# A fused attention and expert stage: head of the schedule written out, attention products in 32-column quarters, one division moved

## The reference, cut to what matters

```python
# experts of the third layer (_L2_ffn_ref), E = 8, K = 2, hidden 512, capacity per expert
h = jax.nn.gelu(jnp.einsum('etc,ehc->eth', toks, fc1_w) + fc1_b[:, None, :], approximate=False)
y = toks + (jnp.einsum('eth,ech->etc', h, fc2_w) + fc2_b[:, None, :]) * layer_scale[:, None, :]
...
# attention of the fourth layer (_L3_xattn_ref), 16 heads of 8, top 32 of 128 keys
scores = jnp.einsum('bhqa,bhka->bhqk', q, k) * SCALE
cutoff = jax.lax.top_k(scores, TOP_K)[0][..., -1:]
w = jax.nn.softmax(jnp.where(scores >= cutoff, scores, -jnp.inf), axis=-1)
e = jnp.einsum('bhqk,bhka->bhqa', w, v)
```

## Time and profile before

| what | us |
|---|---|
| median of 3 timed runs | 3101.04 (3099.99 to 3103.3) |
| the profiled execution, its own time | 3106.62 |
| its span | 3104.8 |
| TensorE busy | 2850.7 (92%) |
| VectorE busy | 2030.3 (65%) |
| ScalarE busy | 1820.0 (59%) |
| GpSimd busy | 1427.0 (46%) |

### The profile page before, as it was taken

How to read it: one execution, slowest core, us unless ns; L and a number is a source line. 1 busy time by engine, 2 the same in 40 slices (tenths; PEclk the granted TensorE clock), 3 DMA queues, 4 the chain that set the end, 5 groups by cost and what they waited for, 6 DMA issues and landing times. The chain is left out here.

```text
span 3104.8 us, 70254 instructions
## 1 busy us (share of the span) xinstructions
PE 2850.7 (92%) x21784; PEld 2265.4 (73%) x21784; DVE 2030.3 (65%) x7995; ACT 1820.0 (59%) x5314; POOL 1427.0 (46%) x1744
## 2 busy tenths in 40 slices
PE   7999979987998989999999998999999996597999
PEld 6888854433775778888888777888888874486676
DVE  4444536764653456666666459999999999486433
ACT  5777734443553356666666567788888873353333
POOL 2122117762542434444444248788888876452000
PEclk9999979987998989999999899899999985597999
DMA  3000024433763311111111000000000000001000
GB/s 114 6 5 6 5 53 85 82 82 112 260 235 95 126 49 54 54 54 54 54 54 54 16 10 14 14 13 13 13 13 13 13 14 32 2 18 36 7 10 10
DMA packets 99460, 151.81 MB, mean 49 GB/s; under 512 B 11312, under 2 KB 39488, under 8 KB 98752
## 3 DMA queue, kind: packets, MB, share of 16 engines
q1 hardware_dynamic: 99296, 149.96, 16.5%
HBM read 103.33 MB, written 46.47 MB: 48 GB/s over the span
## 5 line engine op out<-in xcount | busy, mean ns | idle before, releaser
L1899 POOL TENSOR_TENSOR l2a_probs<-l2a_probs,l2a_inv 128x1024 f32<-128x1024 f32 x128 | 242.3, 1893 | 370.5 <-DVE l2a_inv L2065 370.5
L2010 ACT ACTIVATE l2a_probs<-l2a_s_ps,l2a_nm 128x256 f32<-128x256 f32 x512 | 236.1, 472 | 200.0 <-DVE l2a_nm L2041 200.0
L2760 DVE MAX8 l3a_top<-l3a_work 128x8 f32<-128x128 f32 x1536 | 314.1, 276 | 0.0
L2544 PEld LDWEIGHTS l3a_l2o_ps<-net_arena 128*128 128x128 f32 x2016 | 276.6, 222 | 39.0 <-issue 34.9
L2411 POOL TENSOR_SCALAR l3a_above<-l3a_score,l3a_top 128x128 f32<-128x128 f32 x504 | 294.1, 601 | 16.3 <-POOL l3a_probs L2416 7.2
L2544 PE MATMUL l3a_l2o_ps<-net_arena 128*128 128x128 f32 x2016 | 283.4, 308 | 10.6 <-ACT net_l1f_gate L2620 10.6
L2762 DVE MATCH_REPLACE8 l3a_work<-l3a_top,l3a_work 128x128 f32<-128x128 f32 x1024 | 268.8, 274 | 0.0
L2532 PE MATMUL l3a_l2h_ps<-net_cols,net_arena 128*128 (+1 forms) x1024 | 250.9, 388 | 12.9 <-ACT net_arena L2652 11.2
L2532 PEld LDWEIGHTS l3a_l2h_ps<-net_cols,net_arena 128*128 128x128 f32 x1024 | 184.9, 191 | 65.8 <-ACT net_arena L2652 24.5
L721 ACT ACTIVATE l0a_probs<-l0a_score_ps,l0a_nm 128x128 f32<-128x128 f32 x512 | 179.6, 382 | 73.6 <-DVE l0a_nm L770 73.6
L2652 ACT ACTIVATE net_arena<-l3a_l2h_ps,net_l2f_b 128x256 f32<-128x256 f32 x512 | 210.0, 492 | 16.6 <-PE l3a_l2h_ps L2532 13.7
(11 more groups left out here) (522 smaller groups left out, 7209.1 us busy)
## 6 DMA issues: line engine op xcount, KB each, us to landing
kv_ahead<-l1a_kept SPq DMA_DIRECT2D x128, 256.0 KB, 2.7
l0f_code<-code_rows SPq DMA_DIRECT2D x32, 512.0 KB, 11.5
l2a_kT<-kv_ahead SPq DMA_DIRECT2D x64, 256.0 KB, 2.6
l2a_v<-kv_ahead SPq DMA_DIRECT2D x64, 256.0 KB, 2.6
l1a_shift<-neg_top SPq DMA_DIRECT2D x16, 512.0 KB, 5.0
l1f_chosen<-mask_code SPq DMA_DIRECT2D x64, 128.0 KB, 3.1
keys_ahead<-l1f_keys_kept SPq DMA_DIRECT2D x32, 256.0 KB, 3.3
l3a_kT<-keys_ahead SPq DMA_DIRECT2D x32, 256.0 KB, 2.7
```

Of the source, the lines that this page charges most:

```text
L1899: pool.tensor_tensor(p[:, :, :], p[:, :, :], per_row(inv[c % 2][a][:, :, :].rearrange("p i o -> p (i o)"), KV), ALU.mult).then_inc(scaled, 1)
L2010: act.activation(probs[c % 2][a][:, 2 * i + odd, :], s_ps[a][odd][:, i * KV:(i + 1) * KV], ACT.Exp, bias=nm[c % 2][a][:, i, odd:odd + 1], ...
L2544: ins = pe.matmul(output_bank(u, x)[:, at:at + D], hidden[2 * x + n][:, i, j * P:(j + 1) * P], w2[:, expert(u, 2 * x + n), i, :], start=(i ...
L2760: ins = dve.max(t[:, step // 2, h, :], src)
```

## The change

- **Steps written out.** TensorE and ScalarE start the schedule at c = 0; what stood before it is now a hand-written order. `output` is split in halves of one expert each (`output_half`), which start between the hides. Hidden values of step 1 go to `probs` (`hidden_of`), which is unused then, and the first product of step 1 goes to `s_ps[0]`, so that both need not wait for step 0. `turn_rows` and `norm_rows` of the first group stand ahead of the outputs of step 2.
- **Quarters.** v gets 32 columns per head (8 values, a one, zeros). `apply` loads v and moves the turned probabilities: a head's output is 32 partitions x 128 columns, the four heads of a quarter lie in the four partition quarters of `ov_ps`. When all four are done, ScalarE copies the bank (`take_o`), TensorE transposes it back in four pieces into the same bank (`turn_out`), and `divide` reads it as before, 32 columns apart.
- **The end.** `divide` of tile 29 is done inside the last half of the last search, after its third of seven instructions per head; GpSimd's draining begins with `add_attention`; ScalarE's draining mixes `take_p` and `exps`.

The core of the diff:

```diff
         v_raw = [s.sb(f"v_raw{i}", [P, D]) for i in two]
-        v = [s.sb(f"v{i}", [P, H, DA + 1]) for i in range(4)]
+        WV = 32
+        v = [s.sb(f"v{i}", [P, H, WV]) for i in range(4)]
+        oT = s.sb("oT", [P, BANK])
         qT, kT = s.sb("qT", [P, P]), [s.sb(f"kT{i}", [P, Q4, P]) for i in two]
...
         prefix_ps, total_ps, early_ps = p_ps, ov_ps, s_ps[1]
-        o_ps = ov_ps[:, 0:H * (DA + 1)].rearrange("p (h d) -> p h d", h=H)
+        o_ps = ov_ps[:, :].rearrange("p (h d) -> p h d", h=H)
+        v_blank, o_taken, o_turned = s.sem("v_blank"), s.sem("o_taken"), s.sem("o_turned")
         k_loaded, v_loaded = ([s.sem(f"{n}_loaded{i}") for i in two] for n in "kv")
...
         def output_bank(u, x):
-            return early_ps if (u, x) == (0, 1) else o2_ps
+            return {(0, 1): early_ps, (1, 0): s_ps[0]}.get((u, x), o2_ps)
+
+        def hidden_of(q, u, x):
+            if isinstance(q, int) and (q, u) == (0, 1):
+                flat = probs[x // 2][:, :, :].rearrange("p h s -> p (h s)")
+                size = CHUNKS * WIDE
+                return flat[:, x % 2 * size:(x % 2 + 1) * size].rearrange("p (c n) -> p c n", c=CHUNKS)
+            return hidden[x]
...
                 for t in v:
-                    pool.memset(t[:, :, :], 1.0).then_inc(filled, 1)
+                    pool.memset(t[:, :, :], 0.0).then_inc(v_blank, 1)
+                for i, t in enumerate(v):
+                    pool.wait_ge(v_blank, i + 1)
+                    pool.memset(t[:, :, DA:DA + 1], 1.0).then_inc(filled, 1)
                 pool.wait_ge(filled, 4)
...
                                 (in_group(stage_weights, 0), -AHEAD), (add_attention, 3)], loops=0,
-                         draining=[(for_part(negate_max, 0), 1), (for_part(mask, 0), 1), (add_attention, 3)])
+                         draining=[(add_attention, 3), (for_part(negate_max, 0), 1), (for_part(mask, 0), 1)])
...
                         h = Q4 * n + i
-                        ins = pe.matmul(o_ps[:, h, :], pT[n % 2][:, i, :], v[c % 4][:, h, :], start=True, stop=True)
+                        ins = pe.matmul(ov_ps[WV * i:WV * i + WV, n * P:(n + 1) * P], v[c % 4][:, h, :], pT[n % 2][:, i, :],
+                                        start=True, stop=True)
                     ins.then_inc(av_mm, 1)
+
+                def turn_out(q, c):
+                    wait(pe, o_taken, q, 1, c + 1)
+                    for n in range(NQ):
+                        ins = pe.transpose(ov_ps[:, n * P:(n + 1) * P], oT[:, n * P:(n + 1) * P], k.ident[:, :])
+                    ins.then_inc(o_turned, 1)
...
+                def output_half(q, u, x, n):
+                    wait(pe, act_done, q, 2 * EX, 2 * EX * u + EX * x + 2 * (n + 1))
+                    if n == 0 and (u, x) == (1, 1):
+                        wait(pe, y_ready, q, PARTS, 1)
+                    elif n == 0 and (u, x) not in ((0, 1), (1, 0)):
+                        wait(pe, y_ready, q, PARTS, PARTS * u + x)
+                    for j in range(GT):
+                        at = (n * GT + j) * D
+                        for i in range(CHUNKS):
+                            ins = pe.matmul(output_bank(u, x)[:, at:at + D], hidden_of(q, u, 2 * x + n)[:, i, j * P:(j + 1) * P],
+                                            w2[:, expert(u, 2 * x + n), i, :], start=(i == 0), stop=(i == CHUNKS - 1))
+                    if n == 1:
+                        ins.then_inc(o_mm, 1)
+
                 def output(q, u, x):
-                    wait(pe, act_done, q, 2 * EX, 2 * EX * u + EX * (x + 1))
-                    if (u, x) != (0, 1):
-                        wait(pe, y_ready, q, PARTS, PARTS * u + x)
                     for n in two:
-                        for j in range(GT):
-                            at = (n * GT + j) * D
-                            for i in range(CHUNKS):
-                                ins = pe.matmul(output_bank(u, x)[:, at:at + D], hidden[2 * x + n][:, i, j * P:(j + 1) * P],
-                                                w2[:, expert(u, 2 * x + n), i, :], start=(i == 0), stop=(i == CHUNKS - 1))
-                    ins.then_inc(o_mm, 1)
+                        output_half(q, u, x, n)
+
+                def count():
+                    pe.wait_ge(queue_ready, 2)
+                    flat = queued.rearrange("p i t e -> p (i t e)")
+                    pe.matmul(prefix_ps[:, :], k.upto[:, :], flat, start=True, stop=True).then_inc(counted, 1)
+                    pe.matmul(total_ps[:, :], k.ones[:, :], flat, start=True, stop=True).then_inc(counted, 1)
...
-                for at in range(2 * EX):
-                    hide(0, 0, at)
-                pe.wait_ge(queue_ready, 2)
-                flat = queued.rearrange("p i t e -> p (i t e)")
-                pe.matmul(prefix_ps[:, :], k.upto[:, :], flat, start=True, stop=True).then_inc(counted, 1)
-                pe.matmul(total_ps[:, :], k.ones[:, :], flat, start=True, stop=True).then_inc(counted, 1)
-                output(0, 0, 0)
-                output(0, 0, 1)
-                for at in range(2 * EX):
-                    hide(0, 1, at)
+                def hides(u, first, last):
+                    for at in range(first, last):
+                        hide(0, u, at)
+                hides(0, 0, 5)
+                output_half(0, 0, 0, 0)
+                hides(0, 5, 6)
+                count()
+                output_half(0, 0, 0, 1)
+                hides(0, 6, 8)
+                hides(1, 0, 1)
+                output_half(0, 0, 1, 0)
+                hides(1, 1, 2)
+                output_half(0, 0, 1, 1)
+                hides(1, 2, 5)
+                output_half(0, 1, 0, 0)
+                hides(1, 5, 6)
+                output_half(0, 1, 0, 1)
+                hides(1, 6, 8)
                 turn_weights(0, 0)
+                output_half(0, 1, 1, 0)
                 bias_rows(0, 0)
+                output_half(0, 1, 1, 1)
+                hides(2, 0, 4)
+                turn_weights(0, 1)
+                hides(2, 4, 6)
+                turn_rows(0, 0)
+                hides(2, 6, 7)
+                queries(0, 0)
+                hides(2, 7, 8)
+                scores(0, 0, 0)
+                output(0, 2, 0)
+                scores(0, 0, 2)
+                hides(3, 0, 2)
+                output(0, 2, 1)
+                hides(3, 2, 8)
+                bias_rows(0, 1)
                 schedule(pe, [(for_part(output, 0), 1 - AHEAD), (for_part(hide, 0), -AHEAD), (for_part(hide, 1), -AHEAD),
...
                               (for_part(apply, 2), 2), (for_part(turn_probs, 3), 2), (in_group(turn_weights, 0), -AHEAD),
-                              (for_part(apply, 3), 2), (for_part(scores, 2), -1)], first=2 - AHEAD)
+                              (for_part(apply, 3), 2), (for_part(scores, 2), -1), (turn_out, 2)], first=0)
...
                                    ).then_inc(p_ready, 1)
+
+                def take_o(q, c):
+                    wait(act, av_mm, q, NQ, NQ * (c + 1))
+                    wait(act, o_turned, q, 1, c)
+                    act.activation(oT[:, :], ov_ps[:, :], ACT.Copy).then_inc(o_taken, 1)
...
                     wait(act, h_mm, q, 2 * EX, 2 * EX * u + at + 1)
-                    wait(act, o_mm, q, PARTS, PARTS * (u - 1) + x // 2 + 1)
+                    if not isinstance(q, int) or q or u > 2:
+                        wait(act, o_mm, q, PARTS, PARTS * (u - 1) + x // 2 + 1)
+                    elif u == 2:
+                        wait(act, o_mm, q, PARTS, x // 2 + 1)
                     e = expert(u, x)
                     for n in two:
-                        ins = act.activation(hidden[x][:, 2 * i + n, :], h_ps[i][:, n * WIDE:(n + 1) * WIDE], ACT.Gelu,
+                        ins = act.activation(hidden_of(q, u, x)[:, 2 * i + n, :], h_ps[i][:, n * WIDE:(n + 1) * WIDE], ACT.Gelu,
                                              bias=b1[:, e, 2 * i + n:2 * i + n + 1])
...
-                for u in two:
-                    for at in range(2 * EX):
+                def gelus(u, first, last):
+                    for at in range(first, last):
                         gelu(0, u, at)
+                gelus(0, 0, 8)
+                gelus(1, 0, 6)
                 take_y(0, 0, 0)
+                gelus(1, 6, 8)
+                take_weights(0, 0)
                 take_y(0, 0, 1)
-                take_weights(0, 0)
+                take_y(0, 1, 0)
                 take_bias(0, 0)
+                gelus(2, 0, 1)
+                take_y(0, 1, 1)
+                gelus(2, 1, 4)
+                take_weights(0, 1)
+                norm_rows(0, 0)
+                gelus(2, 4, 6)
+                take_cols(0, 0)
+                take_queries(0, 0)
+                gelus(2, 6, 7)
+                take_scores(0, 0, 0)
+                gelus(2, 7, 8)
+                take_y(0, 2, 0)
+                take_scores(0, 0, 2)
+                gelus(3, 0, 2)
+                take_y(0, 2, 1)
```

(18 more changed lines are left out.)

## The result

The changed kernel takes 3080.57 us (median of four runs, 3078.79 to 3082.22), the kernel before 3102.17 us beside it (four runs, 3099.99 to 3109.42). The ratio is 0.992, 95% interval 0.9905 to 0.9935: 21.6 us faster, where 21.7 were forecast. Measured once more in a later session, the two stood at 3079.77 and 3106.65 us, ratio 0.991 (0.9893 to 0.9928). Two of the executions further down took 3994.92 and 4148.11 us at a mean granted clock of 0.65 and 0.63, and stand in no median and no ratio. The profiled execution took 3081.14 us.

A forecast was written before the change was run, and what follows sets the result against it. The prediction took VectorE's solid block of searches, 816.7 us, as the bound, so only head and tail could move: -8.8 + 0.5 - 13.4 = -21.7 us, from 3101.0 to 3079.3 us, with a spread of 3073 to 3084.

The forecast's parts named there:

- Solid block: Merged stage: VectorE's searches run without waiting, 816.7 us before, 25.5 us a tile; nothing inside counts unless VectorE waits.
- Head: Start of the searches: first search 1806.3, second tile's 1837.0 after a 5.4 us wait; -8.8 us, bounds -6 to -10.5.
- Middle: Tiles between head and tail: TensorE has 1.5 us less per tile, searches stay solid; 0, bounds -0.3 and +8.
- Quarters: Products on TensorE: column groups overlap by 1.9, so 8 passes take 0.5 us, ends 0.25 and 0.94.
- (a): Rival on the quarter products: column quarters don't overlap, 0.94 us each; tail gives 6.5 instead of 13.4; 3086 us; chance 0.14.
- the lower bound of 0.25 us: Quarter products: time of 8 passes if all four column quarters run side by side; the tail's bound of -16 us.
- Tail, the split: After the searches: moved division, draining orders and 2.7 us steps cut 31.8 us by 13.9, taken as -13.4, bounds -16 and -6.5.
- The sum: Whole kernel: -8.8 + 0.5 - 13.4 = -21.7 us, from 3101.0 to 3079.3 us.
- (b): Rival in the middle: turned output reaches the division late, 0.3 us a tile over 27 tiles; 3087 to 3095; chance 0.12.
- (c): Rival in the middle: serial quarters, a 0.16 us drain per shape change; VectorE waits 1.6 us a tile; 3129; chance 0.03.
- (d): Rival at the head: a step waits or TensorE runs at lower clock; tile 1 at 1845, not 1837; 3087; chance 0.06.
- the bound of the head: Limits on the head's gain, -6 to -10.5 us; lower clock after idle in 1794 to 1804 costs up to 3.1.

## Why the forecast came out

- *Solid block:* right for the change, 791.84 us without a wait.
- *Head:* right. First search forecast 1806.3, came at 1806.21; second 1837.0, came at 1837.27; wait ahead of it 5.4, was 5.6. That these agree to 0.3 us is in part luck, since the stretch up to the second search varies by 1.6 us with either head; the mean gain of 8.3 us over the traces is near the -8.8 of the sum. The 1.0 us that I took off for a lower clock was not needed in this trace (the first output behind the scores ran at full clock, 32 instructions in 3.84 us from 1804.99). It is a fair mean all the same: in five of the ten traces with the new head the first search came 1.1 to 2.0 us later in the stage than in the other five.
- *Middle:* the number, 0, was right, its reason was not the whole. The forecast adds head and middle as terms that don't touch each other and takes the quarters' 1.5 us a tile for spare. Without them the head's gain turns into a loss of 8.5 to 20 us of stage (922.90 and 932.31 against 914.35 and 912.56). A layout with one duration for each instruction doesn't show this: the granted clock varies from tile to tile, and so does the reserve, which in the two traces of after is up to 5.0 us and falls to 1.7 and 1.1.
- *Quarters:* overlap right, size off. 0.36 us for eight passes, not 0.50, and 0.58 at the lower clock, not 0.94. A step in the tail is 2.39 us, not 2.7: over eight steps 2.5 us, which is nearly all by which the tail was short (-15.65, forecast -13.4 + 0.5 = -12.9). The trace of before held a nearer row than those that I used, in the attention of the first layer: 32 passes with 128 rows, 64 loaded columns, two column halves by turns, and 128 moving columns.

```profile
382.08 1.97 PE L698 MATMUL l0a_av_ps<-l0a_probs,l0a_v 128*64 128x128 f32 x32
383.97 2.05 PE L653 MATMUL l0a_proj_ps<-net_cols,net_arena 128*128 128x128 f32 x16
```

  The next products start 1.89 us later, 0.059 us a pass, where serial passes take 3.57/32 = 0.112: halves overlap nearly fully at 128 rows. That row spoke against rival (a) and for the lower bound of 0.25 us.
- *Tail, the split:* the total was forecast, its shares are not written out. By the forecast's own terms the quarters give 8 x 0.76 in the steps less two copies and turnings of 1.7 each, 2.7 us, and the order the remaining 11.2 of 13.9. The order alone gave 11.3, the quarters 4.3 more. My 8 for the order, ahead of the run with it alone, was a worse reading of the same layout.
- *The sum:* -21.7 forecast, -25.5 in the profiled pair and in the stage (-23.5 by the second traces), -21.6 in the medians beside it, -26.9 in the second session. That the first pair of medians agrees to 0.1 us is luck, as the start of the stage alone moves by more.
- *Rivals:* (a) fell with the 0.027 us a pass. (b) fell: in both traces each division of the middle had 1.1 us or more to spare. Its mechanism, a small reserve and more time at the lower clock, is what the kernels without quarters show. (c) fell: at most 0.07 us a change where its price was 0.16. (d) fell: tile 1 was searched from 1837.27, and TensorE's granted clock was 1.00 from 1760 to 1810. A small slip stands in the bound of the head: one output at the lower clock costs 6.71 - 3.73 = 3.0 us, not 3.1.

## What to carry to other kernels

An edit whose forecast is "no effect, off the critical path" may be what lets another edit keep its gain: here the quarters alone gave 5 us and were worth some 20 beside the new head. Try two edits together as well as each alone before dropping either. Where an engine is full and another feeds it with a reserve of a few microseconds, count the reserve against the worst granted clock seen in the traces, not its mean: at 0.86 to 0.87 for one tile divisions waited up to 2.9 us. Compare stage lengths cut at the same instructions when the stages ahead of it vary by more than the effect.

## What the runs showed of the hardware

- Products of 32 loaded columns in four column groups with 128 rows and 128 moving columns overlap fully: 0.027 us a pass at 2.4 GHz, and a fixed 0.145 us for a group of them between other shapes (0.053 and 0.157 us at 1.2 GHz). Two groups of 64 columns overlap too, 0.059 us a pass.
- The same loop is granted different clocks in different kernels and executions: over twenty tiles 0.94 and 0.95 in the two traces of after, 0.96 with the quarters alone. With the old products, which fill TensorE nearly to the division, a tile at 0.86 to 0.87 let VectorE wait up to 2.9 us; tiles at 0.90 with 0.97 between them did not.
- The negation behind the last search took 0.16 us in the five traces with the old draining orders and 0.98 to 1.00 us in the nine with the new, where it always meets a `TENSOR_TENSOR` of GpSimd and ends with it (2629.11 + 0.99 = 2630.10, and 2628.80 + 1.27 = 2630.07 above). The Trainium skill (SBUF — State Buffer, section SBUF: two separate sides) says that the two engines share a port pair which the first to start holds for its whole instruction, if VectorE's runs in a 2-port performance mode or has two inputs in SBUF; the trace agrees with the hold, and in which mode the negation (one input) runs it doesn't show. It cost nothing here: ScalarE's exponentials behind it start at 2631.55, after its copies for tile 30, and the negation ended at 2630.10.
